# A four-layer transformer with routed experts on one core: heads of two lengths in turn, tile numbers from row numbers, outputs in tile order, first weights ahead, bias table in another stage

## The reference

```python
# layer 0 and 2, cond: attention, 16 heads of 64, one shared key/value head, one null key, causal, full bias table
sim  = einsum('bhid,bjd->bhij', q, k) + bias      # layer 2: bias from a small MLP over positions (rel_pos_bias)
out  = layernorm(softmax(sim) @ v @ Wo)
# layer 0, ffn: 16 experts, one chosen, 128 places each, relu, 256 -> 1024 -> 256
# layer 1 and 3, cond: 8 gated experts, two chosen, plus one shared gated MLP for every token
scores = softmax(logits);  topk_w, topk_idx = top_k(scores, 2)
y = sum_k topk_w[k] * ((leaky(x @ w_gate[e]) * (x @ w_up[e])) @ w_down[e]);  y = y + shared(x)
# layer 1, ffn: 8 experts, two chosen, gelu, 256 -> 512 -> 256
# layer 2, ffn: product keys and a gated MLP
# layer 3, ffn: rms norm, 8 experts, one chosen, silu, 256 -> 1024 -> 256
```

## Time and profile before

| | us |
|---|---|
| median of 3 runs (lowest, highest) | 3312.52 (3308.84, 3315.05) |
| the profiled execution | 3311.75 |
| its span, first to last instruction | 3309.5 |
| PE busy in it | 2595.6 (78%) |
| PE weight loads busy | 2013.3 (61%) |
| DVE, ACT, POOL busy | 1648.9, 1378.0, 779.8 |

### The profile page before, as it was taken

One profiled execution on the slowest core, in us unless ns is written; L12 is line 12 of the kernel. 1 busy time (PEld: TensorE's weight loads), 2 busy tenths in 40 slices (PEclk: granted clock), 3 DMA queues, 4 the chain that ended last, 5 costly groups with the idle time before them and its releaser, 6 DMA issues. The chain is left out here.

```text
span 3309.5 us, 59545 instructions
## 1 busy us (share of the span) xinstructions
PE 2595.6 (78%) x16144; PEld 2013.3 (61%) x16161; DVE 1648.9 (50%) x4672; ACT 1378.0 (42%) x3221; POOL 779.8 (24%) x1015
## 2 busy tenths in 40 slices
PE   5799999984977533892669999998599997653595
PEld 2467777774966532561346777777577777542585
DVE  3477766643124135222766776664588884315111
ACT  2366666741322221330346666774244441222121
POOL 0032333212023043004123223231233322105001
PEclk9999999996988875996889999999899998895798
DMA  8521212102853574112002122210200001462785
GB/s 300 200 86 59 83 61 86 57 15 81 321 129 115 178 262 162 48 57 81 1 29 84 60 80 64 85 58 15 73 1 0 0 0 36 141 182 84 261 313 179
DMA packets 173776, 341.72 MB, mean 103 GB/s; under 512 B 21830, under 2 KB 125254, under 8 KB 167344
## 3 DMA queue, kind: packets, MB, share of 16 engines
q1 hardware_dynamic: 161328, 307.99, 27.8%
q0 software_dynamic: 12288, 31.83, 3.4%
HBM read 266.71 MB, written 83.17 MB: 106 GB/s over the span
## 5 line engine op out<-in xcount | busy, mean ns | idle before, releaser
L750 DVE CUSTOM_DVE_ANT_0 prob_l<-ps_s,bias_l,nsn 128x1024 f32<-128x1024 f32 (+3 forms) x256 | 277.1, 1083 | 183.9 <-DVEq L749 182.0
L683 PE MATMUL ps_s<-khi,stage 128*128 128x512 f32 (+5 forms) x768 | 342.1, 445 | 10.2 <-POOL stage L657 10.1
L814 ACT ACTIVATE prob_l<-prob_l,nmax 128x1024 f32<-128x1024 f32 (+3 forms) x256 | 252.2, 985 | 66.1 <-DVE nmax L750 63.1
L683 PE MATMUL ps_s<-klo,stage 128*128 128x512 f32 (+5 forms) x768 | 264.1, 344 | 0.0
L950 POOL DMA_INDIRECT yg<-slot_outputs,slot x128 | 131.0, 1023 | 460.1 <-PEq L88 422.2
L677 PE MATMUL ps_s<-km,ident 128*128 128x384 bf16 (+6 forms) x688 | 210.7, 306 | 0.4 <-DVE nmax L750 0.2
L648 POOL COPY nsn<-nsn 128x4 f32 (+1 forms) x128 | 24.1, 188 | 783.3 <-DVE diff L767 650.0
L716 PE MATMUL ps_o<-pT_l,v 128*64 128x256 f32 x1664 | 207.8, 387 | 0.0
L657 POOL TENSOR_TENSOR stage<-qo,stage 64x256 fp32r<-64x256 f32 x256 | 188.4, 736 | 46.9 <-POOLq L656 46.9
L806 ACT ACTIVATE pT_l<-ps_pt 128x512 f32<-128x512 f32 x256 | 152.8, 597 | 99.2 <-PE ps_pt L691 95.9
L1506 ACT ACTIVATE hT<-ps_h,ws 128x128 f32<-128x128 f32 x312 | 89.1, 369 | 238.1 <-PE ps_h L1479 238.1
(11 more groups left out here) (326 smaller groups left out, 5983.6 us busy)
## 6 DMA issues: line engine op xcount, KB each, us to landing
ws<-in_L_ffn_experts_dram SPq DMA_DIRECT2D x39, 2052.0 KB, 7.5
ws<-in_L_cond_experts_dram SPq DMA_DIRECT2D x78, 384.0 KB, 3.4
xs<-slot_rows SPq DMA_DIRECT2D x156, 128.0 KB, 2.0
slot_outputs<-ys SPq DMA_DIRECT2D x156, 128.0 KB, 2.3
slot_rows<-zero_sb SPq DMA_DIRECT2D x1, 17280.0 KB, 53.7
slot_outputs<-zero_sb SPq DMA_DIRECT2D x1, 17280.0 KB, 103.8
bias_l<-in_fside_16xSxS_dram SPq DMA_DIRECT2D x16, 512.0 KB, 3.8
mlp_w<-in_L_ffn_experts_dram SPq DMA_DIRECT2D x8, 1024.0 KB, 18.4
```

Of the source, the lines that this page charges most:

```text
L683: ins = pe.matmul(ps_s[:, u, at:at + hi - lo], stage[:, x.s, x.h % 2, x.h // 2, :], att[part][:, b * S + lo:b * S + hi], start=False, stop ...
L750: dve.tensor_tensor_reduce(out=spans(x, prob), in0=scored(x), in1=spans(x, bias), scale=-1.0, scalar=nsn[:, s, h:h + 1], op0=ALU.add, op1= ...
L814: act.activation(prob[x.s][:, x.h, 0:x.W], prob[x.s][:, x.h, 0:x.W], ACT.Exp, bias=nmax[:, x.s, x.h:x.h + 1], scale=-1.0, accum_out=rsum[: ...
```

## The change

- **Attention core.** Long and short heads alternate: unit `w` has batch `w // 8`, head `w // 2 % 4`, and is short when `w` is odd. Short scores have a bank of their own (`ps_h`), the long ones two double banks (`ps_l`); `ps_o` is one bank for both tiles, and `prob_s` lives in `c["cur"]`. Values of both tiles stand in one place (lag 12), and so does the transposition back (lag 14). Of a long head the second blocks are transposed first, then, after a wait for ACT's copy of the short head, the first four.
- **Tile numbers.** The first tile of each of the 8 experts now has a fixed number `t < 8` and fixed first row `t * T`, with no register load; later tiles read `tile_row`, and in the gated stage the expert is `first // T`. Outputs are stored at `t * P`, in tile order, and the places for gathering are computed from that at the end of routing. `ys_dram` has 39 x 128 rows and is not cleared; `xs_dram` has 16384 rows.
- **First weights.** The weights and biases of the first 4 tiles of both `mlp_experts_phase` are loaded in the routing stage before them.
- **Bias table.** It is computed in `combine_phase` of layer 1, its DVE work mixed with the additions.
- **Routing.** `AHEAD` is 10, the ring 16; the shared MLP's weights have a semaphore of their own.

```diff
 # core_phase
-                self.g, self.b, self.s, self.h = g, w // 8, w // 4 % 2, w % 4
+                self.g, self.b, self.h, self.s = g, w // 8, w // 2 % 4, w % 2
...
+            def turn_short(x):
+                if x.s:
+                    pe.wait_ge(act_s[1].sem, act_s[1].after("exp", x.n))
+                    pe.wait_ge(act_t[0].sem, act_t[0].after("out", x.n - 1))
+                    turn(x, 0, 0, x.qt + 1).then_inc(pe_t[1].sem, 1)
+            def turn_long(x):
+                if not x.s:
+                    pe.wait_ge(act_s[0].sem, act_s[0].after("exp", x.n))
+                    pe.wait_ge(dve_t.sem, dve_t.after("out", x.n - 1))
+                    turn(x, 1, 4, x.qt + 1).then_inc(pe_u.sem, 1)
+                    pe.wait_ge(act_t[1].sem, act_t[1].after("out", x.n))
+                    turn(x, 0, 0, 4).then_inc(pe_t[0].sem, 1)
...
-            units(pe, (0, scores), (9, first_values), (11, second_values), (12, turned_back), (4, transposes))
+            units(pe, (0, scores), (12, all_values), (3, turn_short), (5, turn_long), (14, turned_back))
-            units(dve, (13, outputs), (0, negated), (1, null_differences), (4, second_blocks), (3, totals))
+            units(dve, (15, outputs), (0, negated), (5, second_blocks), (7, null_differences), (10, totals))
-            units(act, (11, outputs), (4, first_blocks), (0, exponentials), (2, null_probability))
+            units(act, (13, outputs), (3, short_blocks), (5, long_blocks), (1, exponentials), (8, null_probability))
 # route_phase
-    AHEAD = 6 if shared is not None else 0
-    RING = 8 if shared is not None else 2
+    AHEAD = 10 if shared is not None else 0
+    RING = NT if shared is not None else 2
...
+            if first_weights is not None:
+                first_weights.load(sp)
...
-            if table:
-                table.vector(dve)
 # finish: what is added at its end, beside a shorter making of the two tables
+                for k in range(choices):
+                    then(dve.tensor_tensor(far[:], oh[:, k], start.unsqueeze(1).to_broadcast([P, NT, E]), ALU.mult))
+                    then(dve.tensor_reduce(pos[:, 0, :], far[:], AX, ALU.add))
+                    then(dve.scalar_tensor_tensor(pos[:, 1, :], rk[:, k, :], float(P), pos[:, 0, :], ALU.is_ge, ALU.mult))
+                    then(dve.tensor_tensor(pos[:, 1, :], pos[:, 1, :], idx[:, k, :], ALU.add))
+                    then(dve.scalar_tensor_tensor(r["slot"][:, k, :], pos[:, 1, :], float(P), rk[:, k, :], ALU.mult, ALU.add))
 def rows_of(eng, r, t):
+    if isinstance(t, int) and t < 8:
+        return t * T
     return eng.value_load(r["tile_row"][0:1, bass.ds(t, 1)], min_val=0, max_val=SLOT_ROWS - P)
 # mlp_experts_phase
+                if isinstance(t, int) and t < 4:
+                    sp.wait_ge(first_weights.sem, 8 * 16)
+                    sp.sem_inc(loads[u], 32)
+                    return
 # glu_experts_phase
-                e = sp.value_load(r["tile_expert"][0:1, bass.ds(t, 1)], min_val=0, max_val=E - 1)
-                sp.dma_start(xs[:, u, :], xs_dram[bass.ds(rows_of(sp, r, t), P), :]).then_inc(loads[u], 16)
+                first = rows_of(sp, r, t)
+                e = first // T
+                sp.dma_start(xs[:, u, :], xs_dram[bass.ds(first, P), :]).then_inc(loads[u], 16)
...
-                first = rows_of(sp, r, t)
                 sp.wait_ge(act_y.sem, act_y.after("y", t))
-                sp.dma_start(ys_dram[bass.ds(first, P), :], ys[:, u, :]).then_inc(stores[u], 16)
+                sp.dma_start(ys_dram[bass.ds(t * P, P), :], ys[:, u, :]).then_inc(stores[u], 16)
 # combine_phase
+            if table:
+                table.positions(gp)
             gather.rows(gp, yg)
...
+            if table:
+                table.vector(dve, rows_added)
+            rows_added(NT)
```

More of the change, by code:

```diff
@@ L544, in core_phase @@
+        ps_h = ph.ps("ps_h", [P, BANK])
         ps_pt = ph.ps("ps_pt", [P, 2, BANK])
-        ps_o = ph.ps("ps_o", [P, 2, BANK])
+        ps_o = ph.ps("ps_o", [P, BANK])
         bias_in = [[ph.sem() for _ in range(4)] for _ in range(2)]
         sp_b = ph.sem()
[L549 to L554, removed]
@@ L555, in core_phase @@
-        act_t = ph.steps("first", 8)
-        dve_t = ph.steps("second", 8)
+        gp_s = [ph.steps("null hi0 waited0 lo0 hi1 waited1 lo1") for _ in range(2)]
+        pe_s = [ph.steps("scores", 8) for _ in range(2)]
+        dve_s = [ph.steps("waited neg", 8) for _ in range(2)]
+        act_s = [ph.steps("exp", 8) for _ in range(2)]
+        pe_t = [ph.steps("turned", 8) for _ in range(2)]
+        pe_u = ph.steps("turned", 8)
+        act_t = [ph.steps("out", 8) for _ in range(2)]
+        dve_t = ph.steps("out", 8)
@@ L562, in core_phase @@
         dve_f = ph.steps("tot rinv nvp")
-        dve_o = ph.steps("ot o")
+        dve_o = ph.steps("ot long short")
         block = ph.stack.enter_context(nc.Block())
@@ new lines, in values, with all_values @@
+                return ins
+            def all_values(x):
+                if x.begins:
+                    pe.wait_ge(dve_o.sem, dve_o.after("ot", x.pair - 1))
+                    pe.wait_ge(act_t[1].sem, act_t[1].after("out", x.n + 3))
+                    values(x, 1, 0, x.tiles[1] + 1)
+                    pe.wait_ge(act_t[0].sem, act_t[0].after("out", x.n + 3))
+                    pe.wait_ge(dve_t.sem, dve_t.after("out", x.n + 3))
+                    values(x, 0, 0, x.tiles[0] + 1).then_inc(pe_v.sem, 1)
@@ L734, in _ @@
                 s.open(dve)
             def negated(x):
-                s, h = x.s, x.h
+                s, h, b = x.s, x.h, x.b
                 if h == 0:
-                    dve.wait_ge(gp_s.sem, gp_s.after("null", x.quad))
-                if s == 0:
-                    dve.wait_ge(pe_u.sem, pe_u.after("second", x.long - 4))
-                else:
-                    dve.wait_ge(pe_t.sem, pe_t.after("first", x.n - 8))
-                if x.b == 0:
-                    dve.wait_ge(bias_in[s][h], (x.pair + 1) * 16)
@@ L1927, in vector @@
         norm("g1", 2)
+        between(2)
         dve.wait_ge(self.turned, 2)
```

434 lines of the change are left out of this document (232 added, 202 removed).

## The result

The changed kernel takes 3199.37 us, median of 4 runs (3195.55 to 3202.59), the kernel before 3312.43 (3308.84 to 3315.05): a ratio of 0.9659, 95% interval 0.9642 to 0.9676. The forecast was 3190, its range 3135 to 3245. The profiled spans, 3197.6 and 3309.5, differ by 111.9 us.

| stages | forecast | before | after | change |
|---|---|---|---|---|
| attention cores 0, 2 | -16 | 539.2, 540.9 | 525.9, 525.3 | -28.8 |
| gated experts 1, 3 | -84 | 141.5, 140.8 | 98.2, 97.1 | -87.0 |
| ffn experts 0, 3 | -31 | 144.0, 215.7 | 131.0, 200.3 | -28.4 |
| routing of layer 1's ffn | -32 | 126.0 | 92.9 | -33.2 |
| combination and null stage | +48 | 45.3, 9.4 | 66.7, 40.7 | +52.7 |

The account below looks back on a forecast made before the run. Bounds were taken stage by stage: PE or its short waits in the cores, SP's issue in the gated experts, single waits in small stages. Terms -84 -16 -31 -32 +48 -7 = -122 from 3311.75 gave 3190, range 3135 to 3245.

Parts of the forecast that it names:

- Gated experts: Both gated stages: SP's issue sets the step, which falls from 3.65 to 2.45 us with one register load; -84 us.
- The 0.15 that I added for limits near by: Gated experts: step taken as 2.45 us instead of the computed 2.3, since SP, transfers and PE lay close.
- rival 2: Gated experts: step ends at 2.95 us, DMA or cold PE replacing SP; 3239; chance 0.15, shared with tile numbers doing nothing.
- First weights: Both ffn expert stages: weights already in place remove most of the starting wait and the second tile's wait; -31 us.
- layer 1's routing: Layer 1's ffn routing: without the bias table on DVE, POOL's scatters follow its gathers without a gap; -32 us.
- the loads cross in routing stages, where SP has nothing else to do: First weights' loads are covered by routing stages; without that cover they cost 30 us each and the gain is nil.
- Combination and null stage: Table work lengthens the combination by 19 us and null stage loads wait behind the spread on SP's queue; +48 us together.
- Rival 1: Null stage: its small loads don't wait for the 8 MB; +20 instead of +48, total 3162; chance 0.17.
- Cores: Both attention cores: fewer waits and handovers for PE, net -0.25 us in each of 64 eight-head spans; -16 us.
- What was taken back (0.65 a span): Attention cores: loss set against the savings, as the long turn waits for ACT's short copy queued near a long exponential.
- Rival 4: Attention cores: PE waits for a long exponential before each short copy, 4.1 us a span, +264; total 3470; chance 0.04.
- Routings ahead of the gated experts: Both cond_moe routings: earlier shared MLP start, AHEAD 10 shifting a few PE tiles, 1.5 us more DVE work; -3 us together.

Follow-up runs that it names:

- null_on_act: Changed kernel with the null stage's four loads in layer 2 issued on ACT's queue, the 8 MB spreading transfer staying ahead on SP's: 3192.99 us.
- spread_after_loads: Changed kernel with the 8 MB bias table transfer issued behind layer 2's null and projection loads: 3172.79 us, ratio 0.9591 to the kernel before.

## Why the prediction was right, and where not

- **Gated experts**, the largest term: right in mechanism and size. SP's register loads set the step; the mean step fell from 3.66 to 2.45, the first eight steps together from 17.9 to 11.9 us (6 for the 5 forecast). That the mean is just the 2.45 forecast is luck in part. I priced a load at 0.67 from the stage's start, which gives 3.65 - 1.34 = 2.3; between undisturbed steps of the loop it is 0.60 (3.00 to 2.40), and 3.65 - 1.20 = 2.45. The 0.15 that I added for limits near by made up for it and had no ground of its own: 2.3 us of transfers was no limit, as the step of 1.72 without a load shows, nor was PE, whose clock came to 0.95 in the stage and whose tile takes 1.54 where I read 1.72 off rows 3. So rival 2 never had the case that I gave it.
- **First weights** and **layer 1's routing**: the starts of 11.4 and the idle time of 31.27 went as worked out. PE now begins 2.0 and 2.6 after xs is issued, and the second wait of 5.6 to 6 is gone. The step "the loads cross in routing stages, where SP has nothing else to do" failed in its second half: SP was free, but the weights came ahead of what the stage waits for first, which came 2.0 and 6.1 later. I had priced only a missing cover (30 us), not the load's own effect on its cover: +6.5, shown by holding it back.
- **Combination and null stage**: +48 forecast, +52.7 measured. The number rests on the spread's landing after 34.2 (37.1 now) and holds for loads in the same queue, where DVE starts about 1 us behind that landing. The reason given, that a queue lands in order, is only a part of it, as `null_on_act` showed. Rival 1 priced sharing the engines at nothing (the wait of 6.13 as before); with the loads on ACT's queue, where they do share, the wait is 29.94.
- **Cores**: -16 forecast, -28.8 measured, inside the bounds but for reasons that I had wrong twice. What was taken back (0.65 a span) I put on ACT; it is DVE's totals, and only in the first pair, the one whose spans grew (16.78 to 16.96). And I let the long score cover the wait for bank 0; alone that brought nothing. The gain hangs on the second blocks being turned first. Start and end of the stage gave another 3.8 in core 0 (28.96 to 27.6 us to the first copy of outputs, 5.34 to 2.9 from the last pair's first copy to the end), which the sum by spans left out. That the total came inside the bounds is no proof of the sum. Rival 4's wait of 4.1 a span did not appear: in all of core 0 the weight loads of the turns wait 6.9 us for ACT's copies of short heads, most of it in the last pair.
- **Routings ahead of the gated experts**: -3 forecast, +8.2 measured. I had the tables' 1.5 us, and wrote that AHEAD = 10 shifts "a few tiles of PE's tail", at no cost. The shift is the cost: with 6 the stages are 13 us shorter together.

The misses, -13 in the cores, +18 in the routings and +5 in the combination and null stage, nearly cancel: the total is 9 off, while the terms one by one are off by over 40. That it came so near is luck.

## What to carry to other kernels

When a stage is bound by a queue's issue, count its register loads: each cost 0.6 to 0.7 us per tile here, and the stage kept yielding down to the last one, beyond the bandwidth that another stage reaches. A prefetch is hidden only if what the covering stage waits for first is in flight ahead of it, or if that wait isn't on the stage's path, as in layer 1's ffn routing: issue large transfers behind the small ones; another queue was no way around it. Where two engines hand a single buffer to and fro, put work that doesn't need the buffer between, and look on which engine the last item ahead of the hand-over is queued.

## What the runs showed of the hardware

- A queue's issue can block: 14.91 us for a small load behind an 8 MB transfer, where it takes 0.35 otherwise.
- Small loads on another queue, issued 2 to 3 us behind the 8 MB, landed 10 to 25 us after their issue, ahead of the 8 MB; with nothing in the way they need 3 to 4 (`spread_after_loads`).
- A register load on SP, with its address arithmetic, costs 0.60 us between undisturbed steps (3.00 to 2.40) and 0.68 for the last one (2.40 to 1.72).
- With no register load on SP, 365 GB/s were reached over 40 us of the gated stage with the DMA engines as good as full, though ffn experts 3 have 278 at 0.76 of the engines' time.
- PE's busy share of the core fell from 98% to 97% while the stage became 13 us shorter: 98% did not mean that PE's work was the limit.
